# One compare for the types and the last keys in the last edge layer of a graph network

## The reference, cut to what matters

```python
W_rel = jnp.matmul(w_comp, V).reshape(num_rels, in_dim, out_dim)
h_src = h[src]
e = jnp.concatenate([z_src, z_e, z_dst], axis=1) @ Wa.T
msg = jnp.einsum('ei,eio->eo', h_src, W_rel[rel_type]) * e
h_out = jax.ops.segment_sum(msg, dst, num_segments=n_nodes)
```

## Time and profile before

| | |
|---|---|
| median of three runs | 3863.26 us |
| the profiled execution's own time | 3856.84 us |
| its span | 3852.9 us |
| outside the span | 3.9 us |
| PE busy | 3468.8 us (90%) |
| DVE busy | 2858.5 us (74%) |
| ACT busy | 1352.5 us (35%) |
| POOL busy | 2106.5 us (55%) |
| mean granted TensorE clock | 0.953 of full speed |

### The profile page before, as it was taken

The page is one execution under the profiler, slowest core; times in us unless marked ns, Lnnn a source line. Parts: engine busy times, 40 slices in busy tenths (PEclk is TensorE's granted clock), DMA queues, the critical chain, the costliest instruction groups (busy, mean ns, idle before and its releaser), DMA issues. The chain is left out here.

```text
span 3852.9 us, 79828 instructions
## 1 busy us (share of the span) xinstructions
PE 3468.8 (90%) x28788; PEld 2039.5 (53%) x28788; DVE 2858.5 (74%) x6620; ACT 1352.5 (35%) x2982; POOL 2106.5 (55%) x2940
## 2 busy tenths in 40 slices
PE   6878877999999978999999999577999999999996
PEld 4656654554455534555555555233566666666564
DVE  8999993233221137888888888456999999999997
ACT  6899980011100003333333333116222222222221
POOL 1000000883000007888888888407888888888886
PEclk8999998999899979999999999778999999999998
DMA  6444437866154383222222222489222222223222
GB/s 167 64 93 64 93 73 323 318 221 249 74 231 176 136 330 78 61 61 62 61 61 63 59 57 57 133 304 369 65 60 55 59 54 55 56 54 58 54 55 43
DMA packets 471493, 453.47 MB, mean 118 GB/s; under 512 B 355445, under 2 KB 402965, under 8 KB 459959
## 3 DMA queue, kind: packets, MB, share of 16 engines
q1 hardware_dynamic: 394582, 400.92, 33.9%
q0 software_dynamic: 50096, 37.33, 5.8%
q10 hardware_dynamic: 26417, 10.05, 1.1%
HBM read 353.92 MB, written 95.85 MB: 117 GB/s over the span
## 5 line engine op out<-in xcount | busy, mean ns | idle before, releaser
L1838 POOL DMA_INDIRECT rows<-typed_table,ring x576 | 662.0, 1149 | 172.8 <-POOL pause L1840 154.0
L2265 PE MATMUL l_ps_g<-ring,h_part 128*128 128x512 f16 x2996 | 719.3, 381 | 14.7 <-DVE ring L2247 14.6
L1420 PE MATMUL L_ps<-ring,L_T 128*128 128x448 fp8e4 (+1 forms) x4606 | 673.8, 389 | 40.3 <-DMA ring<-adj 36.7
L1420 PEld LDWEIGHTS L_ps<-ring,L_T 128*128 128x128 f16 (+1 forms) x4606 | 328.5, 106 | 372.1 <-issue 63.7
L2271 ACT ACTIVATE l_sel<-l_ps_g 128x512 f16<-128x512 f32 x428 | 255.5, 597 | 720.4 <-PE l_ps_g L2265 720.4
L632 PE MATMUL cells<-keys,lows 128*128 128x147 f16 (+5 forms) x2744 | 372.5, 283 | 120.7 <-DVE keys L593 105.0
L2265 PEld LDWEIGHTS l_ps_g<-ring,h_part 128*128 128x128 f16 x2996 | 277.8, 98 | 290.0 <-issue 11.7
L2230 POOL DMA_INDIRECT ring<-typed_table,l_idxA x336 | 371.1, 1104 | 95.6 <-POOL pause L2232 93.9
L1432 DVE SCALAR_TENSOR_TENSOR L_Y<-L_ps,L_scale,dinvB 128x448 f32<-128x448 f32 x84 | 57.4, 684 | 492.9 <-PE L_ps L1420 492.8
L2230 POOL DMA_INDIRECT l_rows<-typed_table,l_idxA x336 | 366.4, 1090 | 99.1 <-POOL pause L2232 98.3
L1900 DVE TENSOR_TENSOR dinvB<-G,tyh 128x1024 f16<-128x1024 f16 x260 | 307.2, 1223 | 127.7 <-ACT G L1887 127.6
(11 more groups left out here) (384 smaller groups left out, 4915.2 us busy)
## 6 DMA issues: line engine op xcount, KB each, us to landing
ring<-adj SPq DMA_DIRECT2D x67, 2744.0 KB, 11.3
adj<-ring SPq DMA_DIRECT2D x14, 2744.0 KB, 9.1
typed_table<-ring SPq DMA_DIRECT2D x49, 765.0 KB, 7.3
ring_fifth<-src_div_mod_rows SPq DMA_DIRECT2D x130, 256.0 KB
l_krow<-src_div_mod_rows SPq DMA_DIRECT2D x107, 256.0 KB
l_trow<-type_row SPq DMA_DIRECT2D x118, 180.0 KB
attr<-in_he POOLq DMA_DIRECT2D x25, 512.0 KB, 6.0
klast<-last_keys SPq DMA_DIRECT2D x86, 128.0 KB
```

What stands on the lines that cost most here:

```text
L1420: ins = pe.matmul(bank[at:at + rows, 0:CH], d["T"][q][:, k, 0:rows], ring[r][:, k, :], start=n < side, stop=n >= NT - side, tile_position= ...
L1838: r_tok_[g] = r_in[b].by(pool.indirect_dma_start(rows[b][:, j, :], None, t1_dram, bass.IndirectOffsetOnAxis(ap=idxA[:, k * SUP + j:k * SUP ...
L2265: ins = pe.matmul(ps_g[p][:, 0:HE], parts[p][:, j, :], hot[b][:, j, h * HE:(h + 1) * HE], start=j == 0, stop=j == GJ - 1)
```

## The change

One tile, `trow`, now holds types in partitions 0 to 89 and the last 24 rows of keys in partitions 96 to 119. One compare over 128 partitions against a new column of constants gives both one-hots in one tile, `tyh`: the multiplier is `rel_scale` in rows 0 to 89 and 1.0 below. The seventh matmul of each gather reads this tile, bf16, in place of the fp16 tile; `expand` reads its rows 0 to 89. The rows of the node table that belong to the last keys move to partitions 96 to 119. The seventh slot of the one-hots and its two memsets are gone. Two memsets on POOL clear `trow` at the start of the layer, and SP waits for them; a memset and a copy of one column are added in `split_relations`.

```diff
+            link(dve, dve.memset(hit_value[:, :], 1.0))
+            step(dve, dve.tensor_copy(hit_value[0:R90, :], rel_scale[:, 3:4]))
...
-            HOT = GJ * SE
+            HOT = (GJ - 1) * SE
...
-            klast = [sb(s, f"l3_klast{b}", [ROWS6, SE], F16) for b in range(2)]
-            trow = [sb(s, f"l3_trow{b}", [R90, SE], F16) for b in range(2)]
-            tyh = [sb(s, f"l3_tyh{b}", [R90, SE], BF16) for b in range(3)]
+            trow = [sb(s, f"l3_trow{b}", [P, SE], F16) for b in range(2)]
+            tyh = [sb(s, f"l3_tyh{b}", [P, SE], BF16) for b in range(3)]
...
-                keys_tok[i] = k_in[b].by(sp.dma_start(trow[b][:, :], type3_dram[:, e].to_broadcast([R90, SE])), 16)
+                keys_tok[i] = k_in[b].by(sp.dma_start(trow[b][0:R90, :], type3_dram[:, e].to_broadcast([R90, SE])), 16)
...
-                    k_in[b].by(sp.dma_start(klast[b][0:LASTK, :], key2_dram[:, e].to_broadcast([LASTK, SE])), 16)
-                    keys_tok[i] = k_in[b].by(sp.dma_start(klast[b][LASTK:ROWS6, :], key1_dram[:, e].to_broadcast([KK, SE])), 16)
+                    k_in[b].by(sp.dma_start(trow[b][LAST_AT:LAST_AT + LASTK, :], key2_dram[:, e].to_broadcast([LASTK, SE])), 16)
+                    keys_tok[i] = k_in[b].by(sp.dma_start(trow[b][LAST_AT + LASTK:LAST_AT + ROWS6, :], key1_dram[:, e].to_broadcast([KK, SE])), 16)
...
-                        dve.wait_ge(*c_x.by(dve.memset(hot[b][:, GJ - 1, :], 0.0)))
...
-                    hot_tok[i] = c_hot.by(dve.tensor_scalar(
-                        hot[b][0:ROWS6, GJ - 1, :], klast[b][:, :], w("at_key")[0:ROWS6, GJ - 1:GJ], None, ALU.is_equal))
...
-                ty_tok[i] = c_ty.by(dve.tensor_scalar(tyh[i % 3][:, :], trow[b][:, :], iotaP[0:R90, :], rel_scale[:, 3:4], ALU.is_equal, ALU.mult))
+                ty_tok[i] = c_ty.by(dve.tensor_scalar(tyh[i % 3][:, :], trow[b][:, :], w("at_type_or_last"), hit_value[:, :], ALU.is_equal, ALU.mult))
...
-                    pe.wait_ge(*hot_tok[i])
+                    pe.wait_ge(*ty_tok[i])
...
-                for j in range(GJ):
-                    ins = pe.matmul(ps_g[p][:, 0:HE], parts[p][:, j, :], hot[b][:, j, h * HE:(h + 1) * HE],
-                                    start=j == 0, stop=j == GJ - 1)
+                for j in range(GJ - 1):
+                    pe.matmul(ps_g[p][:, 0:HE], parts[p][:, j, :], hot[b][:, j, h * HE:(h + 1) * HE], start=j == 0, stop=False)
+                ins = pe.matmul(ps_g[p][:, 0:HE], parts[p][:, GJ - 1, :], tyh[i % 3][:, h * HE:(h + 1) * HE], start=False, stop=True)
...
+            need(sp, *[step(pool, pool.memset(trow[b][:, :], 0.0)) for b in range(2)])
             load_edges(0)
...
+    ws["at_type_or_last"] = np.where(np.arange(P) < LAST_AT, np.arange(P), at_key[:, GJ - 1])[:, None].astype(np.float32)
```

More of the change, by code:

```diff
@@ L50 @@
 REL_TOP = 12
+LAST_AT = 96
 TINY, HUGE = 2.0 ** -100, 2.0 ** 100
@@ L210, in program @@
     rel_scale = sb(life, "rel_scale", [R90, 4])
+    hit_value = sb(life, "hit_value", [P, 1])
     rel2 = rel[:, :, :].bitcast(F16)[:, 0:2, :]
@@ L1710, in gather_plain_tables @@
             for p in range(2):
-                far_tok = s_far.by(act.dma_start(parts[p][LASTK:ROWS6, GJ - 1, :], t["far"]), 16)
+                far_tok = s_far.by(act.dma_start(parts[p][LAST_AT + LASTK:LAST_AT + ROWS6, GJ - 1, :], t["far"]), 16)
             act.wait_ge(*stored)
             s_wide.by(act.dma_start(wide[:, 0:GJ - 1, :], h_dram[0:full, :].rearrange("(j p k) f -> p j (k f)", p=P, k=KK)), 16)
-            tok = s_wide.by(act.dma_start(wide[0:LASTK, GJ - 1, :], h_dram[full:NP, :].rearrange("(p k) f -> p (k f)", k=KK)), 16)
+            tok = s_wide.by(act.dma_start(wide[LAST_AT:LAST_AT + LASTK, GJ - 1, :], h_dram[full:NP, :].rearrange("(p k) f -> p (k f)", k=KK)), 16)
             dve.wait_ge(*tok)
             toks = []
-            for rows, js in ((P, slice(0, GJ - 1)), (LASTK, slice(GJ - 1, GJ))):
-                hi, lo, src = parts[0][0:rows, js, :], parts[1][0:rows, js, :], wide[0:rows, js, :]
+            for at, js in ((slice(0, P), slice(0, GJ - 1)), (slice(LAST_AT, LAST_AT + LASTK), slice(GJ - 1, GJ))):
+                hi, lo, src = parts[0][at, js, :], parts[1][at, js, :], wide[at, js, :]
                 link(dve, dve.tensor_scalar(hi, src, HSCALE - 1.0, None, ALU.mult))
@@ L2085, in relation_layer @@
             flat = [ring[r][:, :, :].rearrange("p k d -> p (k d)") for r in range(RING)]
-            HOT = GJ * SE
-            hot = [flat[b].bitcast(F16)[:, 0:HOT].rearrange("p (j e) -> p j e", j=GJ) for b in range(2)]
+            HOT = (GJ - 1) * SE
+            hot = [flat[b].bitcast(F16)[:, 0:HOT].rearrange("p (j e) -> p j e", j=GJ - 1) for b in range(2)]
             dstP, dstG = ([flat[z].bitcast(F32)[:, HOT // 2 + b * SUP * WIN:HOT // 2 + (b + 1) * SUP * WIN].rearrange("p (e w) -> p e w", e=SUP)
@@ L2137, in relation_layer @@
             c_xkept = Counted(nc, "act_turned")
-            keys_tok, hot_tok, ty_tok, gat, selt, fold_tok, G_tok, w_tok, prod_tok, e_tok, msg_tok, a_tok, sum_tok = ({} for _ in range(13))
+            keys_tok, ty_tok, gat, selt, fold_tok, G_tok, w_tok, prod_tok, e_tok, msg_tok, a_tok, sum_tok = ({} for _ in range(12))
             r_tok_, dst_tok, slot_free, tab_tok, dstg_tok, rows_tok, rt_tok, stored_tok = ({} for _ in range(8))
@@ L2297, in expand @@
                         for p in range(2):
-                            ins = pe.matmul(ps_w[q][:, (j % 2) * 256:(j % 2 + 1) * 256], tyh[i % 3][:, j * P:(j + 1) * P], rel2[:, p, :], start=p == 0, stop=p == 1)
+                            ins = pe.matmul(ps_w[q][:, (j % 2) * 256:(j % 2 + 1) * 256], tyh[i % 3][0:R90, j * P:(j + 1) * P], rel2[:, p, :], start=p == 0, stop=p == 1)
                     if q % 2:
```

## The result

Four runs of the changed kernel took 3831.75 to 3837.73 us, median 3837.28; the kernel before, beside them, had a median of 3866.19 us (3856.84 to 3871.03, four runs). The ratio is 0.9928 [0.991, 0.9946]. I had forecast 3857 us and a range of 3841 to 3876. The profiled execution took 3831.75 us with a span of 3827.9, which is 25.0 us less than before.

The account below looks back on a forecast made before the run. The prediction took POOL's stream of gathers to end the stage. From the median of 3863.3 us it took 6.4 us for POOL's shorter delay, all other terms 0, giving 3857 us, range 3841 to 3876.

Parts of the forecast that it names:

- POOL's gathers ended the stage: Stage of matmul and table groups: POOL's stream of gathers ends it, with some 24 us fixed behind it.
- DVE's 45 us: Line 2247 goes 107 times at 0.42 us on DVE; hidden by PE first and by POOL after.
- PE's step: PE from fold to fold: 10.50 us with a table group and 9.35 us without, expected to stay.
- the seventh matmul with bf16 columns against fp16 weights: PE's gather matmuls, 428 times: cost 0; at the half clock 90 us, a rival with chance 0.02.
- 128 rows cost what 90 do: Line 2251 on DVE: going from 90 to 128 rows costs 0, at most 5 us, hidden.
- the proportional rival: POOL's delay shrinks in proportion to the burst: 17.7 us gained, cut to 17 by PE's floor, 3846 us; chance 0.17.
- the entry (0.24): POOL's gather into which DVE's burst starts loses 0.24 us; claimed to stay unchanged.
- the gather held at the exit (0.94): POOL's gather that meets the burst's end takes 1.89 us, losing 0.94; claimed to stay.
- 107 x 0.06 = 6.4 us: POOL beside a burst 0.42 us shorter: a seventh of that gained a step, the whole forecast gain.
- the lock: Rival: PE's step and DVE's burst settle so each burst's end holds a gather; 25 us slower, 3888 us; chance 0.08.
- The bound of 17 us: Most the change could give with POOL out of the way: PE's gaps, two landing waits, 0.5 us at the start.
- the tail: Stage's end: two waits for landings, 1.47 and 5.16 us, that would go if POOL were out of the way.

Follow-up runs that it names:

- after_dst_first: The changed kernel with the matmul group's one-hot of destinations (line 2256) made ahead of the burst instead of behind it; 3840.99 us in one run.
- long_burst: The changed kernel with an eighth compare of 128 rows put into the burst, its result read by nobody; 3831.69 us, ratio 0.9919.
- long_burst_24: The changed kernel with an eighth compare, on 24 rows and read by nobody, put into the burst; 3851.73 us, ratio 0.9958.
- before_no_last: The kernel before with only line 2247 left out, so the last 24 keys aren't compared; 3844.17 us, ratio 0.9947.
- after: The changed kernel itself, against the kernel before; 3837.28 us, ratio 0.9928.
- compare_in_messages: The changed kernel with an eighth compare of 128 rows put back on DVE outside the burst, among the messages; 3833.76 us, ratio 0.9913.
- long_burst_120: The changed kernel with an unread eighth compare of 128 rows in the burst and the last compare over rows 0 to 119; 3846.16 us in one run.
- long_burst_24_high_b: The changed kernel with an unread eighth compare of 24 rows in the burst, on partitions 96 to 119; 3859.57 us in one run.

## Why the prediction was wrong

**Right:** POOL's gathers ended the stage; DVE's 45 us were hidden; PE's step stayed, so the seventh matmul with bf16 columns against fp16 weights costs nothing; 128 rows cost what 90 do; PE is the next bound. DVE's step was given as 9.83 us while it is ahead. In the changed kernel:

```profile
3120.90 2.55 DVE L2248 TENSOR_SCALAR ring<-l_krow,W 128x1024 f16<-128x1024 f16 x6
3123.37 0.53 DVE L2251 TENSOR_SCALAR l_tyh<-l_trow,W,hit_value 128x1024 bf16<-128x1024 f16 x1
...
3130.74 2.55 DVE L2248 TENSOR_SCALAR ring<-l_krow,W 128x1024 f16<-128x1024 f16 x6
```

9.84 us. My own test was that under 1.20 us of delay a step the proportional rival is right rather than the forecast; it came out at 0.91 (97.9 / 107). The prediction also says that its mechanism is wrong "if the last table gather isn't what the end follows". In the changed kernel that gather starts 15.5 us ahead of PE's last fold, and the end follows PE.

**The step that failed** is "Its two ends stay, and with them the entry (0.24) and the gather held at the exit (0.94)", and from that "0.42 us less of that are 0.06 us a step, 107 x 0.06 = 6.4 us". The term measured 0.41 us a step, 43 us in all. I took the long gather as a fixed price for meeting the exit. But it isn't its length that is fixed, it is its finish: a fixed time after line 2256, the first instruction behind the burst, has started. It lies at 2774.69 us, and line 2256 starts 3.35 us into the burst, there at 2773.19: 1.50 us between them. In the changed kernel it lies at 3567.02 us, line 2256 starts at 3565.52: again 1.50. This holds for 88 of the 91 held gathers before, which start anywhere from 0.8 us ahead of the burst's end to 0.2 behind it (1.49 to 1.54 us), and for all 63 after (1.50 or 1.51).

In the earlier trace rows the gathers start 0.59 us before the burst and 1.29 and 2.96 us into it; the third is the held one. In the changed kernel they start at -0.45, 1.29 and 2.96 us: the third at the same point. With line 2256 0.42 us earlier, it is released 0.42 us earlier: 1.47 for 1.89 us. So stand 57 of the 107 steps before and 63 after. The other steps changed their place in the rhythm as well: the 25 gathers of 1.43 us that started just behind the burst are gone, and 20 now start 0.84 us ahead of its end and take 1.03. No run takes this part from the first; together they come to 0.41 us a step, about what left the burst. I should have asked of the 1.89 us what event ends it; the prediction even gives the distance, and draws nothing from it. It has the lock as well, but only as the rival on the slower side. For the gathers of 1.47 us `after_dst_first` shows that line 2256 is the event. For those of 1.89 no run moved it away; there it is argued from the same 1.50 us.

The proportional rival (17.7 us) named a gain that was too small as well. The Trainium skill's rule behind it ("SBUF — State Buffer", section "Who interferes with whom") is that a `tensor_scalar` in a two-port mode holds the shared pair for the whole instruction and blocks the other side fully. The runs don't bear it out as a price: in `long_burst` the 69 gathers that start 0.06 to 0.07 us into the last compare take 0.95 or 0.96 us, as undisturbed ones do. Its other half is that a `tensor_tensor` with two SBUF inputs contends with GpSimd's reads alone, and that descriptor generation isn't touched (the page calls that inferred). `after_dst_first` shows that such an instruction does hold a gather by an indirect DMA; whether it is POOL's reading of the row numbers in `l_idxA` that waits, no run shows.

**A second cause, in the changed kernel alone.** There the burst has no compare with few rows left, and `long_burst` shows that this by itself would have been enough: eight compares, delay 61 us, and 135 us in `long_burst_24`, which differs in nothing but the rows of one compare. The forecast didn't have it; all I asked of rows was what they cost on DVE. `before_no_last` gains by length alone: its last compare has 90 rows, and the twelve gathers that meet it are still held for 1.89 us. Either cause brings the stage to PE's floor, so they don't add.

**The bound of 17 us was too low**, since 22.1 us came from fold to end. Six kernels (`after`, `before_no_last`, `long_burst`, `compare_in_messages`, `long_burst_120`, `after_dst_first`) end within 1112.2 and 1113.2 us, with 1084.4 us from first to last fold in each, which is the floor. Of it I had PE's gaps (9.9, measured 11.8) but took 6.6 us for the tail, which gave 10.4. Its two waits for landings weren't all: earlier ones had put DVE behind. The scaling at 3818.37 us stood 4.42 us after the last fold; now it stands 1.21 us before it. That is 5.6 us where I took 1.47. From there to the last scaling it is 8.59 us, before 12.17: 3.6 where I took 5.16. The other 1.2 lie behind it.

The range failed for the same reason: its lower end rested on that floor against the median, 3863 - 17 = 3846, with 5 us for spread.

## What to carry to other kernels

When an instruction of one engine is stretched beside a burst of another, find out which event ends it. If its end is tied to the end of the burst, or to what follows it, then what is cut from the burst can come off that instruction in full, not as the fraction by which work inside the burst is slowed. Here it was 0.42 us cut and 0.41 gained a step.

When the engine that ends a stage gives way, the next bound's floor is the whole of its gaps and of the debt that other engines have run up at the end, not the last waits alone. And a cost on the neighbour can hang on an operand's shape that costs its own engine nothing.

## What the runs showed of the hardware

- A gather that starts 0.38 us before the end of a row of fp16 compares takes 0.95 or 0.96 us when the last two have 128 rows, or 128 and 120 (69 of 69 in `long_burst` and in `long_burst_120`). It takes 1.88 to 1.91 us when they have 24 and 90, 96 or 128 (56 to 68 in each kernel), or 128 and 90 (12 of 12 in `before_no_last`). On DVE these compares take the same time. Why is open, and so is whether the number of the rows counts or where they lie.
- A `tensor_tensor` of 128x512 fp32 with two operands in SBUF (0.68 us) holds a gather that starts beside it until 1.50 to 1.61 us after its own start (126 of 126 in the changed kernel): 1.47 us for 0.95 where both start together. One with an operand in PSUM doesn't (184 gathers of 0.94 to 0.97 us).
- It goes the other way too: in `long_burst_24_high_b` a gather that starts 0.1 us ahead of a compare of 128 rows stretches that from 0.55 to 0.71 us.
- A compare on partitions 96 to 119 between compares that start at partition 0 starts 0.08 us late and steps at 0.50 us for 0.42. The Trainium skill, "VectorE: DVE Perf Modes", section "Two Vector instructions with no wait between them", says that an instruction whose input starts in another group of 32 partitions than the last one's is held until all earlier ones have finished. The trace agrees: this compare starts at 3207.17 us, 0.01 us after the six in front of it have ended, and the next 0.02 us after it has, while in the earlier trace rows line 2251 starts 0.07 us before line 2247 has ended. The page gives no price. In the changed kernel all these compares start at partition 0.
- fp16 weights with bf16 columns step like fp16 with fp16: PE's step of 10.51 us holds four such matmuls and is unchanged.
